# The sums of W13's blocks on VectorE instead of GpSimd, with all five orders laid out anew

## The reference, cut to what matters

```python
i, f, g = (einsum('bth,dh->btd', ln(x), W) for W in (Wi, Wf, Wg))
gate = sigmoid(f); v = silu(i) * (1 - gate)
o = scan(o_t = gate_t * o_{t-1} + v_t)            # along t
o = o * rsqrt(mean(o * o) + EPS) * gnorm_w * g * sigmoid(g)
x = x + ln(einsum('btd,hd->bth', o, Wo))
hidden = silu(einsum('bsd,hd->bsh', ln(x), W1)) * einsum('bsd,hd->bsh', ln(x), W3)
hidden = fwht(hidden)                             # Walsh-Hadamard over the 2048 channels
x = x + ln(einsum('bsh,dh->bsd', hidden, W2))
```

## Time and profile before

| | us |
|---|---|
| median of 3 runs (lowest, highest) | 697.42 (695.1, 698.2) |
| the profiled execution, its own time | 695.91 |
| its span in the profile | 694.1 |
| PE busy | 671.3 |
| DVE busy | 464.1 |
| POOL busy | 349.6 |
| ACT busy | 284.1 |

### The profile page before, as it was taken

The page is one execution under the profiler, slowest core; times in us unless marked ns, Lnnn a source line. Parts: engine busy times, 40 slices in busy tenths (PEclk is TensorE's granted clock), DMA queues, the critical chain, the costliest instruction groups (busy, mean ns, idle before and its releaser), DMA issues.

```text
span 694.1 us, 10944 instructions
## 1 busy us (share of the span) xinstructions
PE 671.3 (97%) x4132; PEld 407.3 (59%) x4132; DVE 464.1 (67%) x781; ACT 284.1 (41%) x466; POOL 349.6 (50%) x284
## 2 busy tenths in 40 slices
PE   4999999999999999999999999999999999999996
PEld 2454554444443454548777765566576677777772
DVE  5999899786767667866856554547675644753464
ACT  5988555554453236622422223154133312411231
POOL 1299999999998666753422111125355211311142
PEclk9999999999999999999999999999999999999999
DMA  8945131323457986776477561311556844162103
GB/s 333 406 177 199 52 131 45 107 69 110 160 192 273 225 189 232 265 289 256 122 171 204 202 167 66 109 54 47 197 188 163 218 161 161 53 243 79 59 31 122
DMA packets 58822, 113.31 MB, mean 163 GB/s; under 512 B 33425, under 2 KB 37777, under 8 KB 54161
## 3 DMA queue, kind: packets, MB, share of 16 engines
q1 hardware_dynamic: 58768, 112.61, 49.4%
HBM read 81.92 MB, written 23.07 MB: 151 GB/s over the span
## 4 chain that ended last, share of the span: by engine, by line
PE 61%; POOL 20%; DMA 6%; DVE 4%; issue 4%; SPq 2%; ACT 1%; DVEq 0%; POOLq 0%; ACTq 0%
PE ps L615 20%; PE ps L616 20%; PE ps L617 20%; POOL w2t L1413 4%; DMA ring<-W13t 4%; POOL x1r L1413 4%; POOL rstd L1370 2%; DMA w2t<-W2t 2%; POOL ot L1388 2%; POOL osum L1383 1%; POOL ring L1432 1%; POOL ring L1430 1%; POOL ring L1428 1%; POOL ring L1434 1%; POOL res L1397 1%
## 5 line engine op out<-in xcount | busy, mean ns | idle before, releaser
L615 PE MATMUL ps<-xb,ring 128*128 128x256 f16 (+1 forms) x704 | 225.9, 321 | 3.8 <-DVE ring L1115 1.4
L617 PE MATMUL ps<-xb,ring 128*128 128x256 f16 (+1 forms) x704 | 225.9, 321 | 0.0
L616 PE MATMUL ps<-xb,ring 128*128 128x256 f16 (+1 forms) x704 | 225.9, 321 | 0.0
L1370 POOL TENSOR_TENSOR rstd<-var,neg_half 128x1 f32<-128x1 f32 x64 | 48.1, 757 | 102.5 <-DVE var L1348 37.5
L615 PEld LDWEIGHTS ps<-xb,ring 128*128 128x128 f16 x704 | 69.1, 98 | 51.1 <-issue 4.9
L1438 POOL TENSOR_TENSOR ring<-sga,ring 128x512 f16<-128x512 f32 x36 | 46.7, 1302 | 103.1 <-ACT ring L1029 103.1
L616 PEld LDWEIGHTS ps<-xb,ring 128*128 128x128 f16 x704 | 68.9, 98 | 45.7 <-issue 2.2
L617 PEld LDWEIGHTS ps<-xb,ring 128*128 128x128 f16 x704 | 68.9, 98 | 42.1
L615 PE MATMUL ps<-ring 128*128 128x256 f16 x288 | 78.5, 273 | 0.1
L617 PE MATMUL ps<-ring 128*128 128x256 f16 x288 | 78.5, 273 | 0.0
L616 PE MATMUL ps<-ring 128*128 128x256 f16 x288 | 78.5, 273 | 0.0
(11 more groups left out here) (174 smaller groups left out, 1218.4 us busy)
## 6 DMA issues: line engine op xcount, KB each, us to landing
ring<-w_comb SPq DMA_DIRECT2D x24, 1792.0 KB, 7.5
ring<-W13t SPq DMA_DIRECT2D x16, 512.0 KB, 7.9
ring<-W13t SPq DMA_DIRECT2D x8, 1024.0 KB, 6.2
w_comb<-ring SPq DMA_DIRECT2D x8, 1024.0 KB, 8.6
rows<-L_attn_hidden_states SPq DMA_DIRECT2D x16, 256.0 KB, 4.5
w2t<-W2t SPq DMA_DIRECT2D x8, 512.0 KB, 9.9
res<-L_attn_hidden_states SPq DMA_DIRECT2D x16, 256.0 KB, 5.4
x_rows<-res SPq DMA_DIRECT2D x16, 256.0 KB, 3.5
```

Source lines behind the costliest of these rows:

```text
L615: pe.matmul(dst, a_hi, b_hi, start=start, stop=False)
L616: pe.matmul(dst, a_hi, b_lo, start=False, stop=False)
L617: return pe.matmul(dst, a_lo, b_hi, start=False, stop=stop)
L1370: pool.tensor_tensor(dst, src, neg_half[:].broadcast_to(src.shape), ALU.pow).then_inc(done, 1)
```

## The change

The step SA goes from GpSimd to the DVE: the function `weight_sums` moves from one block to the other with the same four operations, the same operands and the same semaphores. All five tables are replaced. No step is added or dropped on TensorE, ScalarE and SyncE; the DVE's table has eight steps more and GpSimd's eight fewer.

```diff
 PE_ORDER = """
-XT.0.0:4 XT.0.1:5 AN.0.0:6 XT.0.2:7 XT.0.3:0 AN.1.0:1 AN.2.0:2 GC.0.0:3 F.0.0:4 I.0.0:5 F.0.1:6 I.0.1:1 AN.3.0:7
+XT.0.0:4 XT.0.1:5 XT.0.2:6 AN.0.0:7 GC.0.0:0 XT.0.3:1 AN.1.0:2 AN.2.0:3 XT.1.0:4 F.0.0:5 I.0.0:7 G.0.0:6 G.0.1:1
...
 DVE_ORDER = """
...
+S.1.3 UP.0.5 WT.10.0 WT.10.1 UP.0.6 WT.11.0 WT.11.1 WT.12.0 P.1.3 UP.0.7 WT.12.1 WT.13.0 WT.13.1 WT.14.0 UP.0.8
+SA.0.0 MS.1.0 UP.0.9 WT.14.1 H2.0.1 H2.1.0 H2.1.1 SO.0.0 UP.0.10 H2.2.0 WT.15.0 Y.1.0 Y.1.1 WT.15.1 SA.1.0
...
         @block.vector
...
+            def weight_sums(j, _):
+                dve.wait_ge(ld_s, 16 * (j + 1))
+                a11, a12, a21, a22 = quad(0, 0), quad(0, 1), quad(1, 0), quad(1, 1)
+                dve.tensor_tensor(a22, a21, a22, ALU.add).then_inc(sa_rdy, 1)
+                dve.wait_ge(sa_rdy, 4 * j + 1)
+                dve.tensor_tensor(a21, a11, a21, ALU.subtract).then_inc(sa_rdy, 1)
+                dve.wait_ge(sa_rdy, 4 * j + 2)
+                dve.tensor_tensor(a11, a22, a11, ALU.subtract).then_inc(sa_rdy, 1)
+                dve.wait_ge(sa_rdy, 4 * j + 3)
+                dve.tensor_tensor(a12, a12, a11, ALU.subtract).then_inc(sa_rdy, 1)
...
         @block.gpsimd
...
-            def weight_sums(j, _):
-                pool.wait_ge(ld_s, 16 * (j + 1))
...
```

More of the change, by code:

```diff
@@ new lines @@
+XT.1.1:2 W2N.0.0:3 AN.3.0:5 XT.1.2:7 F.0.1:0 F.0.2:4 I.0.1:6 W2N.1.0 I.0.2:5 I.0.3:6 G.0.2:0 G.0.3:2 W2N.2.0
+XT.1.3:1 W2N.3.0 F.0.3:4 F.1.0:5 I.1.0:7 G.1.0:1 I.1.1:4 I.1.2:0 MS.0.0:6 Y.0.0:2 Y.0.1:5 Y.0.2:7 WS.0.0:1
+W2N.4.0 Y.0.3:6 F.1.1:4 W2N.5.0 W2N.6.0 W2N.7.0 F.1.2:1 G.1.1:2 I.1.3:5 ZT.0.0:7 W2S.0.0:3 F.1.3:6 G.1.2:4
+ZT.0.1:1 ZT.0.2:2 ZT.0.3:0 G.1.3:7 GA.0.0:1 UP.0.0:2 GA.0.1:0 UP.0.1:1 GA.0.2:6 UP.0.2:0 GA.0.3:2 H2.0.0:1
+UP.0.3:3 GA.0.4:6 H2.0.1:0 UP.0.4:2 GA.0.5:4 UP.0.5:5 GA.0.6:3 H2.1.0:1 UP.0.6:6 GA.0.7:2 UP.0.7:4 GA.0.8:5
@@ new lines @@
+D.2.49 GQ.3.2:7 GR.3.2:4 GQ.3.3:6 D.2.50 D.2.51 D.2.52 D.2.53 GR.3.3:7 D.2.54 D.2.55 GU.3.2:5 GP.3.4:4 D.2.56
+GP.3.5:5 GQ.3.4:4 GU.3.3:6 GP.3.6:5 D.2.57 GQ.3.5:7 D.2.58 D.2.59 D.2.60 D.2.61 D.2.62 D.2.63 GR.3.4:4 GR.3.5:6
+GU.3.4:7 GP.3.7:5 GU.3.5:4 D.3.0 GQ.3.6:7 GQ.3.7:5 GP.3.8:6 D.3.1 D.3.2 D.3.3 D.3.4 D.3.5 D.3.6 GR.3.6:7
+GU.3.6:4 D.3.7 D.3.8 D.3.9 GR.3.7:6 GU.3.7:5 D.3.10 D.3.11 D.3.12 GQ.3.8:7 D.3.13 D.3.14 D.3.15 GP.3.9:4
+GR.3.8:6 GQ.3.9:5 D.3.16 GU.3.8:4 GP.3.10:7 D.3.17 D.3.18 GR.3.9:5 GU.3.9:7 D.3.19 GQ.3.10:6 GR.3.10:5 D.3.20
@@ new lines @@
+D.3.21 D.3.22 GP.3.11:4 GQ.3.11:7 GR.3.11:6 GP.3.12:4 GQ.3.12:7 GP.3.13:5 GQ.3.13:4 D.3.23 D.3.24 GU.3.10:6
+D.3.25 GU.3.11:5 D.3.26 D.3.27 D.3.28 GP.3.14:6 GQ.3.14:5 D.3.29 GR.3.12:7 GR.3.13:6 D.3.30 D.3.31 GU.3.12:7
+D.3.32 D.3.33 GP.3.15:7 D.3.34 D.3.35 GU.3.13:4 D.3.36 D.3.37 D.3.38 GR.3.14:7 D.3.39 D.3.40 GQ.3.15:6 GR.3.15:4
+GU.3.14:5 GU.3.15:7 D.3.41 D.3.42 D.3.43 D.3.44 D.3.45 D.3.46 D.3.47 D.3.48 D.3.52 D.3.56 D.3.60 D.3.49 D.3.53
+D.3.57 D.3.61 D.3.50 D.3.54 D.3.58 D.3.62 D.3.51 D.3.55 D.3.59 D.3.63
@@ L167 @@
+UP.3.10 UP.3.11 UP.3.12 UP.3.13 UP.3.14 UP.3.15 V.3.0 V.3.1 V.3.2 V.3.3
 """
 SP_ORDER = """
[L170 to L173 removed]
@@ L1442, in v @@
                 rsqrt(rstd[:, 3, t:t + 1], var[:, 3, t:t + 1], v_rstd)
-            run(pool_steps, {"X1": x1, "S": sum_squares, "P": gated, "Y": y, "YN": yn, "Z1": z1, "FW": pool_butterfly, "ZA": row_sums, "SA": weight_sums, "UP": up,
+            run(pool_steps, {"X1": x1, "S": sum_squares, "P": gated, "Y": y, "YN": yn, "Z1": z1, "FW": pool_butterfly, "ZA": row_sums, "UP": up,
                  "V": v})
```

242 lines of the change are left out of this document (108 added, 134 removed).

## The result

The changed kernel takes **694.7 us** (692.7 to 697.4), the kernel before beside it 696.7 us (694.5 to 698.9), 20 runs of each. The ratio is 0.997, with an interval of 0.996 to 0.9985: faster by 2 us or 0.3%, less than the 0.5% that the prediction called no change. The forecast was 701.5 us and slower. The time lies inside the range of 692.5 to 709, but near its lower end and on the other side of zero.

The account below looks back on a forecast made before the run. TensorE bounds the kernel, its work unchanged. Terms +6.4 - 0.3 - 0.9 - 0.9 = +4.3 us take the profiled 695.9 to 700.2; with 1.5 for the median, forecast 701.5 us, range 692.5 to 709.0.

Parts of the forecast that it names:

- What would show it: List of signs, among them GA.0.0 near 108.8 us, idle over 1 us ahead of Y.0.0 and a transpose near 98.
- part C: The sums moved from GpSimd to the DVE: -0.3 us up to D.0.0, plus -0.9 for the wait at 255.83.
- The credit of 1.6 us: TensorE's waits at 209.98 and 213.28 us, ahead of D.0.0, would go: -1.6 us.
- the debit of 1.3 us: UP.0.13, standing behind SA.2.0 on the DVE, would be late for H2.6.1: +1.3 us.
- Parts A and B: The start and the stretch up to the first hidden product: GA.0.0 at 108.8 against 102.4, +6.4 us, bounds +3 to +9.
- HB ahead of the splits: Hidden bound placed before batch 0's last splits on the DVE, one WT moved behind: +2.3 us for the last split.
- The DVE's new pauses: DVE waits ahead of GA.0.0 for a tile, ScalarE's AT.2.0 and G.0.2, and I.1.0: +2.6 us.
- The Y.0.0 wait: TensorE would come to Y.0.0 at about 70 us and start near 73, idle over 1 us, inside the +6.4.
- part A: The start up to I.0.0: later F.0.0 (21.0 against 19.74) and I.0.0 at 24.6, +1.7 us.
- Part D: Third batch's attention: waits of 0.4 and 0.6 replace 1.12, half clock at even odds, -0.1 - 0.8 = -0.9 us.
- The wait at 256 us: TensorE's wait at 255.83, from UP.0.15 behind SA.5.0 on GpSimd, would go: -0.9 us.
- The DVE keeps up: Rival: early loss only +0.3, total -5.0, 692.4 us, if the last split ends by 102.5 us; chance 0.18.

Follow-up runs that it names:

- tiny_before: The kernel before with each SA operation on GpSimd cut to two columns (128x2), rest of the sums left out; 691.07 us, ratio 0.991.
- orders_alone: The changed kernel with the eight SA back on GpSimd, all five new orders kept; 710.95 us, ratio 1.022 to the kernel before.
- hb_back: The changed kernel with the hidden bound HB behind the last split ZT.0.3 again; 693.41 us, ratio 0.997 to the kernel before.
- move_gap: The kernel before with the eight SA on the DVE at chosen places, SA.2.0 in the DVE's pause ahead of YN.1.3; 694.59 us, ratio 0.996.
- start_old_hb: The changed kernel with the old order up to F.0.0 on TensorE, ScalarE and DVE, and HB behind the splits; 694.52 us, ratio 0.996.
- move_placed: The kernel before with the eight SA on the DVE, each placed after its load landed, with SO.2.0 three steps later; 694.78 us, ratio 0.998.
- after_again: The changed kernel run again unaltered, with a second trace; 694.84 us, ratio 0.997 to the kernel before.

## Why the prediction was wrong

**Sums in it.** The five waits that it lists add up to 5.0 us, not 4.5, and 695.9 + 4.3 + 1.5 gives 701.7, not 701.5; neither changes the reading.

**What held.** TensorE is the bound; its busy time is the same, and nothing waits behind 303 us. The waits at 53.56, 209.98, 213.28 and 255.83 went, as it said. GA.0.0 is late, 107.1 against the forecast 108.8. Of *What would show it* the idle ahead of a transpose near GA.0.0 is there.

**The step that failed: part C.** It counted -0.3 us at D.0.0. TensorE gained 3.1 between GA.0.0 and D.0.0 (110.8 to 107.8 us), and tiny_before gains 2.7 in the old orders by nothing but lighter sums. The mechanism, GpSimd's relief against the DVE's load, was the right one; two terms were mis-sized. The credit of 1.6 us took only the two waits that stand last ahead of D.0.0; the idle time of the old kernel between GA.0.0 and them, some 1.2 us in small pieces, belonged for the most part to the same lateness of GpSimd, since tiny_before has lost them. And the debit of 1.3 us, a late UP.0.13 behind SA.2.0, didn't come: I had priced the first three SA at 5.6 us, and SA.2.0 took 2.9. That it didn't come is the work of the new orders: in the old ones the sums on the DVE do cost TensorE 3.4 to 3.8 us here (111.6 and 112.0 against the 108.2 of tiny_before). The DVE's groups for the four operations of SA, all eight pairs:

```profile
L1273 DVE TENSOR_TENSOR ring<-ring 128x512 f32<-128x512 f32 x8 | 7.4, 929 | 0.3
L1271 DVE TENSOR_TENSOR ring<-ring 128x512 f32<-128x512 f32 x8 | 7.3, 915 | 0.3
L1269 DVE TENSOR_TENSOR ring<-ring 128x512 f32<-128x512 f32 x8 | 6.6, 830 | 0.3
L1267 DVE TENSOR_TENSOR ring<-ring 128x512 f32<-128x512 f32 x8 | 5.5, 688 | 3.4 <-DMA ring<-W13t 3.4
```

SA.0.0 and SA.1.0 took 4.7 and 4.8 us, near my figure, and six of the eight took 2.9 to 4.0. The Trainium skill ("SBUF — State Buffer", "Who interferes with whom") has the two engines lock each other out for a whole instruction. The single operations agree: 0.69 us, or 1.5 to 1.8 beside a GpSimd operation of 128x512. What I left out is that work taken off GpSimd no longer meets the DVE's other operations: they became 7 to 8 us shorter by the move, some 0.3 of what the sums cost. The new orders took 11 us more off them (orders_alone). So the 20.1 us of room that I had set against a cost of 17 grew, by the move and more so by the orders.

**Parts A and B: right in kind, too large.** Together +6.4, measured +4.7, and +3.3 without the landing's luck. HB ahead of the splits was right in place, at 1.5 to 1.9 of the 2.3 us. The DVE's new pauses did come, and longer than the 2.6 us forecast: 2.7 us for one AT alone, 1.0 at a split of the second batch, 1.7 for the gated product.

```profile
45.82 0.75 DVE L1115 SCALAR_TENSOR_TENSOR ring<-ring,row_s 128x512 f16<-128x512 f32 x1 [2.73 <-ACT ring L881]
...
63.65 0.75 DVE L1168 SCALAR_TENSOR_TENSOR sg<-sg,g_coef,o_s 128x512 f32<-128x512 f32 x1 [1.74 <-ACT sg L926]
```

Wrong was to add them to a DVE as full as before. It is not: from 40 to 60 us it is busy 15.91 us against 19.93, and from 12 us to GA.0.0 78.3 against 83.2; its operations are shorter there, an AT 0.93 us on average from 8 to 60 us against 1.12. The Y.0.0 wait didn't come: the eight matmuls of the mean square start at 71.96 and Y.0.0 at 72.77 with none. F.0.0 was forecast at 21.0 and started at 22.9. XT.0.3 ended on the DVE at 22.2 in place of 21.0, since the tile ahead of it landed at 19.0 and not at 17.7. TensorE itself came 0.7 us later still, without a wait, and part A had left out two things on its way: the 2.4 us that it stands at GC, and the lower clock: the four bf16 matmuls of AN.2.0 start 0.45 us apart in the changed kernel and 0.22 in the old one. I had written that a lower clock early on was not counted.

**Part D** was -0.9, of it -0.8 for half a chance of the clock. The wait is 1.3 in place of 1.1, and the clock gave 1.7 in this pair of traces; over many executions a lower mean clock goes with 1.8 us in more than half of the old kernel's, as said above. **The wait at 256 us** was right, -0.9 against -1.1.

Put together from the two traces: +4.7 at GA.0.0, -3.1 to D.0.0, -1.1 at 256, -1.7 behind MS.2.0: -1.2, which is the difference of the spans, 692.9 and 694.1. Against the forecast of +4.3 that is 5.5 us less: 2.8 of it in part C, 1.7 in parts A and B (3.1 if the landing is taken out, as much as part C), the rest in part D and at 256. The medians differ by 2.0 because the profiled execution of before was 0.8 us shorter than its median (695.9 against 696.7; its landing at 11.3 is early) and that of the changed kernel 0.3 longer (695.0 against 694.7). The interval of the ratio allows 1.0 to 2.8 us.

**The choice among the rivals.** None of them is what happened. *The DVE keeps up* had the right sign for another reason: it asked for the last split by 102.5 us, and the last split ended at 106.0 (forecast: 107.4). The case that came, an early loss of 3 us that TensorE's free run behind it more than pays for, was missing, since the relief stood in the sum with 1.2 us. All the rows for it were there: GpSimd at 98.1 of 100 us, and what the DVE waits for in the old kernel shows GpSimd behind TensorE's waits.

**No version beats the changed kernel** for certain: hb_back, move_gap, start_old_hb and it lie within 694.6 +- 1.2 us, their intervals over each other. What can be shown is that the move to the DVE, well placed in the old orders, gives the same total (move_placed), so the new orders add nothing to it in sum: what they win up to D.0.0 they lose ahead of GA.0.0. And tiny_before (0.991 against 0.997) shows that some 4 us more would be there for who finds room for the sums that costs nobody anything.

## What to carry to other kernels

An idle time names the engine that released it last, not the one that was late: before pricing a relief, follow the named engine's own waits one step back, or shrink the work in place to two columns, which gives the price of the whole relief in one run. When elementwise work goes from GpSimd to the DVE, count what it costs there less what the DVE's other two-input operations get back (here 27 us less 7 to 8). Where the moved step stands is worth more than the move: it brings its wait for a load along, and the same eight steps cost 8 us ahead of others' work and gain 2 in the pauses.

## What the runs showed of the hardware

- A sum of 128x512 f32 on the DVE takes 0.69 us, or 1.5 to 1.8 beside a GpSimd operation of the same size; cut to 128x2 it still takes 0.16 to 0.29 on average. On GpSimd the same is 1.27 us in single rows and 1.35 to 1.39 on average at full width, and 0.20 to 0.31 at two columns.
- With 40 to 47 us of work taken off GpSimd, the DVE's other operations became 7 to 8 us shorter in all: 6.8 us in tiny_before (457.3 against 464.1), 7.0 in move_placed, 8.3 in move_gap.
- The first use of a weight differs by 1.8 us between executions (AN.0.0 from 11.3 to 13.1 us), mostly by its landing, as much as the whole effect that was measured. One trace of each kernel can't place an effect of that size at the start.
- In after_again, the second trace of the changed kernel, with a wait of 3.0 us at GC, two stretches behind it have a granted clock of 0.50:

```profile
17.00:18.90 1.90, 1.90 (x6) 0.43 (x4) 0.95 (x4) 1.90 (x3) 0.00 (x0) 0.50 0.63 237
18.90:20.50 1.60, 1.60 (x5) 0.43 (x4) 1.49 (x6) 1.60 (x4) 0.95 (x2) 0.50 1.02 348
```

In the first trace the same matmuls start as far apart, 0.45 us, while the column says 1.00: at the very start the spacing of matmuls tells the clock, and the column may not.
